# Moving the degree counts of a hypergraph layer under its gathers and scatters, in a four-layer graph network on one core

## The reference, cut to what matters

```
deg_n = segment_sum(ones, src, N)          # how often each node is a source
Dinv  = where(deg_n > 0, 1 / deg_n, 0)
deg_e = segment_sum(ones, dst, 10000);  Binv = where(deg_e > 0, 1 / deg_e, 0)
he  = Binv * segment_sum((x @ W)[src], dst, 10000)
out = Dinv * segment_sum(he[dst], src, N) + b
```

## Time and profile before

| what | us |
|---|---|
| median of 3 runs | 3143.76 (3129.03 to 3147.51) |
| the profiled execution | 3136.22 |
| its span | 3134.4 |
| layer 0 within the span | 0 to 669.9 |

### The profile page before, as it was taken

One profiled execution on the slowest core, in us unless ns is written; L12 is line 12 of the kernel. 1 busy time (PEld: TensorE's weight loads), 2 busy tenths in 40 slices (PEclk: granted clock), 3 DMA queues, 4 the chain that ended last, 5 costly groups with the idle time before them and its releaser, 6 DMA issues. The chain is left out here.

```text
span 3134.4 us, 48304 instructions
## 1 busy us (share of the span) xinstructions
PE 2077.7 (66%) x10165; PEld 1475.8 (47%) x10165; DVE 2139.2 (68%) x8782; ACT 1682.8 (54%) x4590; POOL 1582.2 (50%) x1489
## 2 busy tenths in 40 slices
PE   3673534637767778788745788777776666664665
PEld 1332512525545656666632334343335655564555
DVE  5798523338877888898857777777745544444999
ACT  2592101238874656565647988898965444442222
POOL 3200565520007888888827666655607777774000
PEclk9896767879996677666767999999998888877999
DMA  2497422449997787787747999999966555554998
GB/s 72 146 360 304 80 56 75 101 114 323 322 306 264 243 249 230 244 255 234 235 103 216 290 290 286 283 294 286 292 170 216 178 186 181 181 175 137 316 316 280
DMA packets 494677, 696.59 MB, mean 222 GB/s; under 512 B 66363, under 2 KB 357398, under 8 KB 485932
## 3 DMA queue, kind: packets, MB, share of 16 engines
q1 hardware_dynamic: 416414, 511.30, 51.5%
q0 software_dynamic: 63360, 130.75, 15.6%
q10 hardware_dynamic: 14736, 52.96, 4.7%
HBM read 394.91 MB, written 327.18 MB: 230 GB/s over the span
## 5 line engine op out<-in xcount | busy, mean ns | idle before, releaser
L274 POOL DMA_INDIRECT xs<-x_d,table_src x400 | 386.7, 967 | 350.1 <-DVE x L1502 128.4
L274 POOL DMA_INDIRECT xs<-n_d,srcI x200 | 240.1, 1201 | 325.6 <-DVEq L1151 270.4
L274 POOL DMA_INDIRECT xd<-n_d,dstI x200 | 235.4, 1177 | 60.9 <-issue 54.5
L274 POOL DMA_INDIRECT xd<-x_d,table_dst x200 | 211.4, 1057 | 65.1 <-issue 64.5
L1860 PE MATMUL bank<-xs,same 128*128 128x129 f32 x400 | 109.2, 363 | 180.7 <-ACT sums L1829 93.0
L1721 POOL DMA_INDIRECT r_d<-rd,out_row x200 | 196.5, 982 | 60.9 <-issue 60.9
L1657 PEld LDWEIGHTS bank<-nmsg,same 128*128 128x128 f32 x400 | 61.4, 193 | 267.7 <-ACT sums L1589 209.0
L1657 PE MATMUL bank<-nmsg,same 128*128 128x128 f32 x400 | 99.9, 333 | 130.2 <-ACT sums L1589 74.9
L269 ACT ACTIVATE root<-tmp,eps 128x4 f32<-128x4 f32 (+3 forms) x253 | 76.8, 303 | 196.4 <-DVE tmp L245 195.8
L250 DVE RECIPROCAL rs<-root 128x4 f32<-128x4 f32 (+3 forms) x253 | 51.9, 205 | 185.5 <-ACT root L269 173.2
L474 POOL DMA_INDIRECT sum_d<-add,to x40 | 62.5, 1563 | 228.4 <-ACT add L663 187.7
(11 more groups left out here) (393 smaller groups left out, 7131.5 us busy)
## 6 DMA issues: line engine op xcount, KB each, us to landing
n_d<-T SPq DMA_DIRECT2D x98, 528.0 KB, 3.8
nt<-n_d SPq DMA_DIRECT2D x49, 1056.0 KB, 7.3
r<-r_d SPq DMA_DIRECT2D x98, 520.0 KB, 5.5
bc<-dst_d SPq DMA_DIRECT2D x170, 256.0 KB, 4.6
r_d<-nv SPq DMA_DIRECT2D x49, 528.0 KB, 7.7
v_d<-nv SPq DMA_DIRECT2D x49, 528.0 KB, 7.7
nv<-v_d SPq DMA_DIRECT2D x49, 528.0 KB, 4.3
x_d<-x SPq DMA_DIRECT2D x100, 256.0 KB, 4.8
```

The source lines that it names most:

```text
L274: pool.indirect_dma_start(out=out, out_offset=None, in_=table, in_offset=bass.IndirectOffsetOnAxis(ap=index, axis=0)).then_inc(s, 16)
```

## The change

- 50 steps (and 2 that count padding) in place of 52, sources and destinations apart. **Sources:** two steps per group in the first gathers (the first with bank 1 too), three per group in the first scatters, then `m` = 2 more; they use ACT's signs as before. **Destinations:** three steps per group in the second gathers, two per group in the second scatters, 2 more; both halves on DVE.
- `finalize` is split: `of_sources` behind the first scatters, `of_sources_behind` and `places` after it, `of_destinations` behind the second scatters. The table is stored twice, each time at the end of a scatter stage on SP; the second gathers wait for the first store.
- `sum1_d` is zeroed by 16 copies of 1.6 MB from the zero padding of `x`, issued by ACT right after the first loads. ACT copies `x` to `x1_d` at the start of the second convolution.
- Setup waits for 8 first loads (and one more for `K0`); 10 others go to ACT's queue, 10 stay on SP, 9 follow the stores of `src_d`, `dst_d`. POOL's first two groups of gathers wait for `src_ready` alone. ACT's and PE's lists still hold the weight work, behind all of `loads`, ahead of the first signs and the first histogram matmul.
- In the first gathers the scale comes ahead of the masks on DVE.

```diff
                 def _(sp):
-                    for dst, src in plan:
+                    for dst, src in first_plan:
+                        sp.dma_start(dst, src, allow_slow_non_contiguous=True).then_inc(first_loads, 16)
+                    sp.dma_start(K0[:, :], t["consts"][:, K_COLS:K_COLS + Z_COLS]).then_inc(k0_in, 16)
+                    for dst, src in plan[10:20]:
                         sp.dma_start(dst, src, allow_slow_non_contiguous=True).then_inc(loads, 16)
                     sp.wait_ge(columns_in, 1)
                     for k, table in ((0, src_d), (1, dst_d)):
                         sp.dma_start(table.rearrange("(a r p) -> r a p", a=2, p=P), rowsF[:, k, :, :]).then_inc(rows_out, 16)
+                    for dst, src in plan[20:]:
+                        sp.dma_start(dst, src, allow_slow_non_contiguous=True).then_inc(loads, 16)
...
                         bounded(sp, n, load_back)
+                        sp.wait_ge(meta_ready, conv + 1)
+                        sp.dma_start(meta_d.rearrange("(p l) m -> p (l m)", p=NHI),
+                                     meta[:, :, :].rearrange("p l m -> p (l m)")).then_inc(meta_out, 16)
+                        if conv == 0:
+                            sp.wait_ge(firsts_ready, 1)
+                            sp.dma_start(first_d.rearrange("(a r p) -> r a p", a=2, p=P), firsts[:, :, :]).then_inc(rows_out, 16)
...
                 def _(pe):
-                    pe.wait_ge(loads, 16 * len(plan))
+                    pe.wait_ge(first_loads, 16 * len(first_plan))
...
+                    pe.wait_ge(loads, 16 * len(plan))
+                    nc.tensor.transpose(bank[4][:, 0:D], wq[:, :], ident)
...
                         def sums(g, s):
                             if conv == 0:
-                                histogram(g, s, True)
+                                sources(g * 2, 0, True)
+                                sources(g * 2 + 1, 1)
...
+                            if conv == 1:
+                                for k in range(3):
+                                    destinations(g * 3 + k, (s + k) % 2)
...
                             last.then_inc(e["he_ps"], 1)
+                            if conv == 0:
+                                sources(n * 2 + g * 3, s)
...
-                        lagged(pe, n, hyperedges, combined)
+                        def counted(g, s):
+                            for k in range(2):
+                                if conv == 0:
+                                    sources(n * 2 + g * 3 + (k + 1), (s + k + 1) % 2)
+                                else:
+                                    destinations(n * 3 + g * 2 + k, k)
+                        lagged_thirds(pe, n, hyperedges, combined, counted)
...
                 def _(act):
                     act.preload_act_table(ACT.Sqrt)
+                    act.sem_inc(q[0]["h_ready"], 2)
+                    for dst, src in plan[0:10]:
+                        act.dma_start(dst, src, allow_slow_non_contiguous=True).then_inc(loads, 16)
+                    act.wait_ge(first_loads, 16 * len(first_plan))
+                    for k in range(16):
+                        act.dma_start(sum1_d[k * ZERO:(k + 1) * ZERO, :].rearrange("(p r) f -> p (r f)", p=96),
+                                      t["x"][N:N + ZERO, :].rearrange("(p r) f -> p (r f)", p=96)).then_inc(zeroed, 16)
                     act.wait_ge(weights_ps, 1)
...
+                        if conv == 0:
+                            def signed(g, s):
+                                for k in range(2):
+                                    signs(n * 2 + g * 3 + (k + 1), (s + k + 1) % 2, n * 2 + g * 3 + (k + 1))
+                            lagged_thirds(act, n, rows_of_edges, additions, signed)
+                            m = steps_behind(act)
+                            def behind(i, b):
+                                signs(n * 5 + i, b, n * 5 + i)
+                            bounded(act, m, behind)
+                            additions(n - 1, 1)
+                            act.wait_ge(deg_ready, 1)
+                            nc.scalar.activation(a["root"][:, :], a["w"][:, :], ACT.Sqrt).then_inc(root_ready, 1)
...
                     def stages(conv):
+                        if conv == 1:
+                            act.sem_inc(e["h_ready"], 2)
+                            for k in range(NX // COPY):
+                                act.dma_start(x1_d[k * COPY:(k + 1) * COPY, :].rearrange("(p r) f -> p (r f)", p=P),
+                                              t["x"][k * COPY:(k + 1) * COPY, :].rearrange("(p r) f -> p (r f)", p=P)).then_inc(x_copied, 16)
```

More of the change, by code:

```diff
@@ L36 @@
 NN = NHI * NLO
[L37 to L39 removed]
+NH = NT // G
+NTP = (5 * NGE + NH - 20) * G
+NX = 52 * 8 * P
 NGN = NN // (P * G)
@@ L122, in lagged, with lagged_thirds @@
     second(count - 1, 1)
+def lagged_thirds(eng, count, first, second, third):
+    first(0, 0)
+    third(0, 0)
+    first(1, 1)
+    second(0, 0)
+    third(1, 1)
+    with eng.Fori(2, count - 1, 2) as i:
+        first(i, 0)
+        second(i - 1, 1)
+        third(i, 0)
+        first(i + 1, 1)
+        second(i, 0)
+        third(i + 1, 1)
 def lagged_by_two(eng, count, first, second):
@@ L604, in _, with signs @@
                     act.wait_ge(set_up, 1)
[L606 to L607 removed]
+                    def signs(k, b, at):
+                        hold("act", act, hot_used, k + 1)
                         for j in range(G):
[L609 to L610 removed]
+                            last = nc.scalar.activation(lows[:, b, j, :], iota[:, :], ACT.Sign,
+                                                        bias=split["ls"][:, bass.ds(at * G + j, 1)])
                         last.then_inc(lows_ready, 1)
@@ new lines, in sources @@
+                    def sources(k, b, at, of_low=False):
+                        dve.wait_ge(hot_used, k + 1)
+                        for j in range(G):
+                            for part, hi in enumerate(("hs", "hl") if of_low else ("hs",)):
+                                last = nc.vector.tensor_scalar(hot[:, b, j, part * NHI:(part + 1) * NHI], iota[:, 0:NHI],
+                                                               split[hi][:, bass.ds(at * G + j, 1)], None, ALU.is_equal)
+                        last.then_inc(hot_ready, 1)
@@ new lines, in destinations @@
+                    def destinations(k, b):
+                        dve.wait_ge(col_used, k + 1)
+                        for j in range(G):
+                            at = bass.ds(k * G + j, 1)
+                            nc.vector.tensor_scalar(hot[:, b, j, 0:NHI], iota[:, 0:NHI], split["hd"][:, at], None, ALU.is_equal)
+                            last = nc.vector.tensor_scalar(lows[:, b, j, :], iota[:, :], split["ld"][:, at], None, ALU.is_equal)
+                        last.then_inc(col_ready, 1)
@@ L928, in reached @@
                             nc.vector.reciprocal(binv[:, s, :], binv[:, s, :]).then_inc(e["binv_ready"], 1)
+                            for k in range(2):
+                                if conv == 0:
+                                    sources(n * 2 + g * 3 + (k + 1), (s + k + 1) % 2, n * 2 + g * 3 + (k + 1))
+                                else:
+                                    destinations(n * 3 + g * 2 + k, k)
                             if conv == 0:
@@ L935, in stages, with behind @@
                         bounded(dve, n, reached)
+                        m = steps_behind(dve)
+                        def behind(i, b):
+                            if conv == 0:
+                                sources(n * 5 + i, b, n * 5 + i)
+                            else:
+                                destinations(n * 5 + i, b)
+                        bounded(dve, m, behind)
                         nc.vector.tensor_copy(last_cols[:, :], last_low[:, bass.ds((n - 2) * G, 2 * G)]).then_inc(e["last_cols_ready"], 1)
+                        if conv == 0:
+                            of_sources(m)
+                        else:
+                            of_destinations(m)
                         dve.wait_ge(e["last_ps"], 1)
```

295 lines of the change are left out of this document (154 added, 141 removed).

## The result

The changed kernel takes 3170.04 us (median of 4 runs, 3164.0 to 3174.55) beside 3145.29 us for the kernel before (4 runs): ratio 1.009, interval [1.0057, 1.0122]. It is about 25 us (0.9%) slower; the forecast was 3135 us, 2 us faster in the profiled execution's own count. Profiled span against profiled span the difference is 3172.7 - 3134.4 = +38.3 us. The last scatter of layer 0 is issued at 694.1 us against 661.0, so 33 of these lie in layer 0 and 5 in the layers behind it, which the change does not touch.

A forecast was written before the change was run, and what follows sets the result against it. In each of six stages of layer 0 another resource works without rest. Terms of +46, 0, -150, +22, +68, +7, +2 and +3 sum to -2 us against 3136.2: 3135 us, 8 in 10 range 3065 to 3190.

The forecast's parts named there:

- Part 1: Setup up to the first ReLU: loads complete only behind the zeroing; first ReLU at 99 against 52.6 us, +46 us.
- Part 2: First gathers, first ReLU to last eviction: 8.3 us per group against 8.7 before; 0, between -5 and +8 us.
- Part 3: Stretch from 137.0 to 294.4 us, between first gathers and first scatters: falls to 7.3 us, -150 us.
- Part 4: First scatters: a new loop through ACT and PE, 12.4 us per group against 10.0; +22 us, between +17 and +60.
- Part 5: Last `to` to the second convolution's first mask: mask stands behind the x copy, at +103 against 35 us; +68 us.
- part 6: Second gathers: DVE's third step waits for PE, 11.8 us per group against 11.07, +7 us; steps ahead of `across`, +2.
- Part 7: Second scatters: two steps per group fit in POOL's 10.5 us; only those before the first scatter count, +3 us.
- The handoff: First gathers: a root-scale handoff of about 1 us, within the 8.3 us per group.
- Small DMAs get through: Rival for setup and x copy: first ReLU at 27 us (-72), first mask at +45 (-58); 3005 us, chance 10%.
- One copy hidden: Rival: zeroing or x copy is hidden, or both in part; 3065 to 3077 us (-58 or -72), chance 17%.
- Rival 3: PE falls to 1.2 GHz in the loops of first scatters and second gathers, +76 us; 3211 us, chance 12%.
- the likeliest case: The forecast itself, whole kernel: 3135 us, own range 3105 to 3165, chance 60%.

The follow-up runs named there:

- a shorter standstill ahead: Changed kernel with the x copy paced: three copies at the old point, ten behind each group's ReLU in the second gathers; ratio 1.0008.
- sparser counting: Changed kernel with two steps of destinations per group in the second gathers and three in the second scatters; 3485.07 us, ratio 1.0108.
- the new order: Changed kernel with TensorE's and ScalarE's work in the first scatters in another order; ratio 1.0053 to the kernel before.
- the control: The changed kernel again, unedited, on another chip, against the kernel before there; ratio 1.0115.

## Why the prediction was wrong

The waits it named held, and no part went against its sign; the loss comes from sizes. Forecast and measured, in us:

| part | forecast | measured |
|---|---|---|
| 1 setup and zeroing | +46 | +51.8 |
| 2 first gathers | 0 | -5.3 |
| 3 the stretch | -150 | -148.5 |
| 4 first scatters | +22 | +30 |
| 5 up to the first mask | +68 | +74.4 |
| 6 second gathers; tail | +7; +2 | +22.4; 0 |
| 7 second scatters | +3 | +8 |
| other layers | 0 | +5 |
| sum | -2 | +38 |

**The step that failed is TensorE's time in the loops of parts 4 and 6**, "With 0.9: 12.4 us per group" and "at 0.85 11.8 us". 13.7 and 13.56 us were measured, and the two parts together missed by 21 of the 40 us by which the sum was off. Both stages had a mean granted clock of 0.75, and I had argued 0.9 and 0.85 from the share of TensorE's busy time, between two stages of the earlier trace rows; the trace after has the first gathers at 1.00 with TensorE busy 80% of the time and the first scatters at 0.75 with 70%. With 0.75 the formula of part 4 gives 5.55 + 6.2/0.75 = 13.8 us, that of part 6 5.8 + 5.1/0.75 = 12.6, and the whole forecast 3135 + 17 = 3152.

But the mean is not a clock at which anything ran. One group of the first scatters (two rows), one of the second gathers (two rows, and TensorE's timeline in it):

```profile
312.50:319.00 6.50, 5.91 (x19) 3.92 (x20) 2.39 (x12) 4.81 (x8) 4.66 (x3) 0.50 0.41 36
319.00:323.20 4.20, 3.89 (x31) 3.39 (x29) 2.02 (x13) 1.31 (x5) 0.00 (x0) 0.99 0.06 6
473.50:480.00 6.50, 6.43 (x8) 2.65 (x9) 3.17 (x15) 0.00 (x0) 5.01 (x5) 0.54 0.39 102
480.00:481.10 1.10, 1.10 (x6) 0.62 (x5) 0.00 (x0) 0.00 (x0) 0.80 (x2) 1.00 0.06 3
```

```profile
473.57 6.62 PE L575 MATMUL bank<-mask,h 128*128 128x512 f32 x8 [3.00 <-DVE mask L969]
480.03 1.89 PE L557 MATMUL bank<-lows,hot 128*98 128x512 bf16 x8
481.20 0.25 DVE L839 TENSOR_SCALAR hot<-iota_b,sp_hd 128x98 bf16<-128x98 f16 x1 [4.53 <-PE bank L557]
```

In these groups, and likewise in four others of the second gathers and two of the first scatters, the clock goes between 0.50 and 1.00. After TensorE has waited 3.0 us (second gathers) or 3.3 us (first scatters) for its inputs it works at 0.50, and only some 6 us later at 1.00. The terms that come first pay for it. In part 6 these are the sums: 4.1 us at full clock by my terms, 4.8 in the forecast, and measured over the stage

```profile
L575 PE MATMUL bank<-mask,h 128*128 128x512 f32 x72 | 58.7, 990 | 120.0 <-DVE mask L969 120.0
```

58.7/9 = 6.5 us a group. That is 1.7 of the 1.76 us by which the period was missed; the fixed terms, VectorE's, were about right (13.56 - 6.5 - 1.1 for the step leaves 6.0 us, forecast 5.8). In part 4 the second step and `hyperedges`, 2.8 us at full clock, took 4.6 in the group shown, and the step and `combined` behind them, at 0.99, 3.3 as priced. That the loop of VectorE and TensorE sets the period of part 6 is shown (two steps instead of three: 100.0 us); what the clock took of it is read from the rows and not from a run that changed the clock alone. What decides the clock in a stage stays open: a shorter standstill ahead did not raise its mean (0.73), sparser counting (0.79) and the new order (0.82) went with a higher one.

Part 4 has a second slip that cancelled: the earlier trace rows are 10.2 us apart and not 10.0, and they are the fastest of the stage. From the first scatter to the ninth the mean period was 10.8 us before and 13.9 after, so eight periods of 3.1 us make 25, where I had seven of 2.45.

**Part 1** was right in what it depends on: the weight work stands behind `loads`, and these behind the zeroing. The last copy landed at up to 18.1 + 74.3 = 92.4 us, not 86: the bulk moved 21.39 MB in 66 us, 324 GB/s, where I had reckoned with 25.95 MB in 77 us, 337. The transposes came at 96, not 90.

**Part 5** likewise: of 27.26 MB the copy had moved 27.07 by 425 us, so it ended some 104 us behind the last `to` (forecast 101), and the mask followed at 109.6 (forecast 103). I had looked for `bc` as the last one. It was the gathered table rows, since GpSimd had waited 43.83 us for the landing of the last scatters before it could gather.

**Part 2** came out 5 us below its forecast and at its bound. From the first ReLU to the tenth it is 69.3 us, 7.7 a group (8.7 before, 8.3 the forecast's own term), and from there to the last eviction 9.8 us (6.5 before), at a clock of 1.00 where the stage had 0.92. The handoff of about 1 us that I had charged does not appear in the period.

**Part 3** held within 2 us. **Part 7**: the first scatter comes 4.9 us later (forecast 3), and the scatters, forecast at nothing, take 3.4 us more. That the added steps are the reason is likely, not shown; with three steps a group instead of two it was 108.1 us beside the control's 107.3.

**The rivals.** *Small DMAs get through* is refuted by the packets, 632 against 658. *One copy hidden* did not happen. Rival 3, TensorE slow in the loops, was the right side and not the right size: it priced all of TensorE's terms at twice their time, and in the groups read above some ran at 0.50 and the others at 1.00. No run shows the 2.4 and 1.2 GHz that stand in the sums of parts 4 and 6 and in this rival; the traces give the granted clock as a share, and a step of four matmuls took 1.91 us at 0.50 (from 312.56 us) and 1.03 us at 0.99 (from 319.63 us). A case of its own was missing in between. The range (3065 to 3190) held the result; the likeliest case's own range (3105 to 3165) ended 5 us short.

## What to carry to other kernels

Price a bulk transfer by what waits beside it: turns that the small queue needs (packets on its busiest engine) times the length of a turn, and at most the bulk's own duration. (An estimate: in the setup the cap and the count came out alike, and only the stretch with 16-KB packets shows the length of a turn at work by itself.) Cut it into small pieces and place these where the engines, not the transfers, set the pace (26 MB in 9-KB rows cost the gathers 3.3 us, in 64-KB packets in one go 44); never in front of loads (79 us of setup, and with 17-KB packets in the same place the first ReLU came at 107.2 us against 108.9), or of a wait that ends a stage (16.6 us for `bcd` behind two copies, 6.1 with them behind the first two groups). When work moves into a loop of two engines, write the loop as fixed part plus TensorE's part, and read the granted clock under each of TensorE's terms in windows of a few microseconds, not as the mean of a stage: here a mean of 0.75 hid sums at 0.54, and this was the largest of the errors.

## What the runs showed of the hardware

- SyncE's issue instruction itself stood up to 24.8 us for one broadcast of 128 rows beside 64-KB packets (up to 14.8 in the control), up to 7.8 us beside 17-KB ones, and 0.43 us without bulk: issuing is not free beside bulk, and everything behind it on the queue waits too.
- A 26-MB zeroing at a DMA share of 0.96 and 367 GB/s, from zeros on the chip, in rows of 9 KB and spread over the groups, cost the gathers beside it 3.3 us; the same amount copied in 64-KB packets in one go cost 44.
- The granted clock was 1.00 in gathers with TensorE busy 80% of the stage, and 0.75 in scatters with 70% and in gathers with 69%. The 0.75 of the latter is made of stretches at 0.50 and at 1.00 within a group: 0.54 to 0.59 under the sums (6.3 to 6.5 us, five groups), 1.00 under the step behind them (two groups). A step of four matmuls took 1.03 us at 0.99 and 1.91 us at 0.50.
- Beside the x copy and the zeroing, packets of the small queue and of the bulk passed nearly one for one: 144 beside 176, 658 beside 632, 1360 beside 1357. The time of such a turn was 2.15 and 1.67 us beside 64-KB packets and 0.78 us beside 17-KB ones.
